# An LSTM step on one core: the new cell in PSUM for ScalarE's tanh, and a second copy of it in SBUF at the end of the step

## What is computed

```python
xW = jnp.einsum('ntd,dg->ntg', x, Wx) + b
def step(carry, xw_t):
    prev_h, prev_c = carry
    a = xw_t + prev_h @ Wh
    i = jax.nn.sigmoid(a[:, :Hdim])
    f = jax.nn.sigmoid(a[:, Hdim:2 * Hdim])
    o = jax.nn.sigmoid(a[:, 2 * Hdim:3 * Hdim])
    g = jnp.tanh(a[:, 3 * Hdim:])
    next_c = f * prev_c + i * g
    next_h = o * jnp.tanh(next_c)
    return ((next_h, next_c), next_h)
_, hs = jax.lax.scan(step, (h0, c0), jnp.swapaxes(xW, 0, 1))   # h0 is cond_1024, c0 is zero
x = x + jnp.swapaxes(hs, 0, 1)
```

## Time and profile before

| | before |
|---|---|
| median of 3 executions | 1871.62 us (1871.56 to 1872.72) |
| the profiled execution's own time | 1872.67 us |
| its span, from the first to the last instruction | 1870.8 us |
| VectorE busy | 1766.2 us, 94% |
| TensorE busy | 1691.8 us, 90% |
| ScalarE busy | 1084.4 us, 58% |
| mean granted TensorE clock | 0.999 |

### The profile page before, as it was taken

How to read it: one execution, slowest core, us unless ns; L and a number is a source line. 1 busy time by engine, 2 the same in 40 slices (tenths; PEclk the granted TensorE clock), 3 DMA queues, 4 the chain that set the end, 5 groups by cost and what they waited for, 6 DMA issues and landing times.

```text
span 1870.8 us, 104928 instructions
## 1 busy us (share of the span) xinstructions
PE 1691.8 (90%) x45116; PEld 1064.5 (57%) x45116; DVE 1766.2 (94%) x9739; ACT 1084.4 (58%) x3985; POOL 168.8 (9%) x536
## 2 busy tenths in 40 slices
PE   1899999999999999999999999999999999999997
PEld 0555555555555555555555555555555555555554
DVE  8999999999999999999999999999999999999998
ACT  4555555555555555555655555555655555556554
POOL 0000000000000000000000000000000000000000
PEclk9999999999999999999999999999999999999999
DMA  5000000000000000000000000000000000000000
GB/s 208 15 26 21 21 25 21 21 21 26 21 21 26 21 21 23 24 21 21 26 20 20 26 21 21 21 26 21 21 26 21 21 23 23 21 21 26 18 12 14
DMA packets 39058, 48.96 MB, mean 26 GB/s; under 512 B 4416, under 2 KB 36160, under 8 KB 38592
## 3 DMA queue, kind: packets, MB, share of 16 engines
q1 hardware_dynamic: 37152, 37.77, 6.4%
q10 hardware_dynamic: 1440, 4.49, 0.6%
HBM read 25.46 MB, written 16.78 MB: 23 GB/s over the span
## 4 chain that ended last, share of the span: by engine, by line
DVE 76%; PE 21%; issue 2%; DMA 1%; ACTq 0%; DVEq 0%
DVE turned L500 21%; PE acc L301 12%; DVE mailbox L504 12%; DVE products L513 10%; PE acc L307 8%; DVE o_gate L518 6%; DVE h_halves L529 4%; DVE gates L523 4%; DVE h_halves L538 4%; DVE h_feat L533 3%; DVE x_halves L483 3%; DVE out_ring L565 3%; DVE o_preact L508 3%; DVE x_tops L576 2%; DMA wh<-in_wh 1%
## 5 line engine op out<-in xcount | busy, mean ns | idle before, releaser
L301 PE MATMUL acc<-wh_low,h_halves 128*32 128x256 f16 x16384 | 719.6, 274 | 134.4 <-DVE h_halves L529 132.1
L307 PE MATMUL acc<-wh_high,h_halves 128*32 128x256 f16 x16384 | 724.9, 275 | 0.2
L250 ACT ACTIVATE gates<-mailbox 128x96 f32<-128x96 f32 x1024 | 256.3, 250 | 639.6 <-DVE mailbox L504 639.6
L293 PE MATMUL x_acc<-wx_high,x_halves 128*32 128x512 f16 x8192 | 621.0, 380 | 1.1 <-ACT x_acc L224 1.1
L301 PEld LDWEIGHTS acc<-wh_low,h_halves 128*32 128x32 f16 x16384 | 389.7, 96 | 395.0 <-DVE h_halves L529 381.8
L500 DVE STREAM_TRANSPOSE turned<-acc 128x256 f32<-128x256 f32 x1024 | 458.1, 447 | 58.0 <-PE acc L307 52.1
L307 PEld LDWEIGHTS acc<-wh_high,h_halves 128*32 128x32 f16 x16384 | 343.5, 96 | 132.4 <-DVE h_halves L538 6.8
L293 PE MATMUL x_acc<-wx_low,x_halves 128*32 128x512 f16 x4096 | 399.1, 379 | 0.0
L227 ACT ACTIVATE acc<-x_acc,step_mask 128x512 f32<-128x512 f32 x512 | 328.4, 642 | 3.9 <-PE x_acc L293 3.9
L184 POOL TENSOR_TENSOR o_preact<-turned 128x32 f32<-128x32 f32 x512 | 165.6, 323 | 1696.8 <-DVE turned L500 1696.8
L504 DVE TENSOR_TENSOR mailbox<-turned 128x96 f32<-128x96 f32 x1024 | 269.9, 264 | 17.6
(11 more groups left out here) (66 smaller groups left out, 534.8 us busy)
## 6 DMA issues: line engine op xcount, KB each, us to landing
out<-out_ring SPq DMA_DIRECT2D x128, 128.0 KB, 2.1
x_ring<-in_x SPq DMA_DIRECT2D x120, 128.0 KB, 2.9
wx<-in_wx ACTq DMA_DIRECT2D x4, 512.0 KB, 8.1
wx<-in_wx SPq DMA_DIRECT2D x4, 512.0 KB, 8.1
wh<-in_wh SPq DMA_DIRECT2D x4, 512.0 KB, 16.7
wh<-in_wh ACTq DMA_DIRECT2D x4, 512.0 KB, 17.0
x_ring<-in_x SPq DMA_DIRECT2D x2, 512.0 KB, 16.5
b_rows<-in_b ACTq DMA_DIRECT2D x1, 256.0 KB, 21.2
```

The lines of the kernel that those rows point to most:

```text
L250: act.activation(gates[par][n][:, 1:4, :], preact[n].rearrange("p (g c) b -> p g (c b)", c=2), ACT.Tanh, scale=rescale[chunk % 2]).then_in ...
L293: last = pe.matmul(x_acc[pair % 2][32 * j:32 * j + 32], x_halves[:, pair % (CHUNK // 2), c, half], w[:, c].rearrange("p (n q) g -> p q n g ...
L301: pe.matmul(acc[par][32 * j:32 * j + 32, n, 0:GL], h_halves[1 - par][:, c, 0:2], w_low["wh"][:, c, n * Q + j], start=False, stop=False, sk ...
L307: last = pe.matmul(acc[par][32 * j:32 * j + 32, n, 0:GL], h_halves[1 - par][:, c, 1:3], w_high["wh"][:, c, n * Q + j], start=False, stop=c ...
```

## The change

VectorE's new_cell now writes the cell to PSUM, into the tile `cell[n]` in `mailbox[n]`, and ScalarE's tanh reads it there. Two more VectorE instructions, `keep_cell(0)` and `keep_cell(1)`, compute the cell again from the same products and write it to SBUF, where the next step's gate_products reads it. They stand behind low_of_h(1) and ahead of the output row. They signal a new semaphore, `cell_kept`, for which gate_products(0) of the next step waits beside its wait for ScalarE. Group 1's `preact` moves to `mailbox[1]`, and the wait for `x_sum_ready` in step 6 moves up, ahead of add_three(1).

```diff
-        preact = [mailbox[0][:, 96 * n:96 * (n + 1)].rearrange("p (k b) -> p k b", b=B) for n in range(NG)]
+        preact = [mailbox[n][:, 0:96].rearrange("p (k b) -> p k b", b=B) for n in range(NG)]
+        cell = [mailbox[n][:, 128:128 + 2 * B] for n in range(NG)]
...
+        cell_kept = sem("cell_kept")
...
-                    act.activation(cell_tanh[n], gates[1 - par][n][:, 0, :], ACT.Tanh, scale=0.5)\
+                    act.activation(cell_tanh[n], cell[n], ACT.Tanh, scale=0.5)\
                         .then_inc(h_parts_ready[n], 1)
...
                 def gate_products(n):
+                    if t > 0 and n == 0:
+                        dve.wait_ge(cell_kept, NG * t)
                     dve.wait_ge(gates_ready, nth[n])
...
                 def new_cell(n):
                     dve.wait_ge(products_ready, nth[n])
+                    dve.scalar_tensor_tensor(cell[n], products[n][:, 0, :], 0.5, products[n][:, 1, :],
+                                             ALU.mult, ALU.add).then_inc(cell_ready, 1)
+
+                def keep_cell(n):
                     dve.scalar_tensor_tensor(gates[1 - par][n][:, 0, :], products[n][:, 0, :], 0.5, products[n][:, 1, :],
-                                             ALU.mult, ALU.add).then_inc(cell_ready, 1)
+                                             ALU.mult, ALU.add).then_inc(cell_kept, 1)
...
                 gate_products(0)
+                if at == 6 and chunk + 1 < CHUNKS:
+                    dve.wait_ge(x_sum_ready, chunk + 2)
                 add_three(1)
...
                 high_of_h(0)
-                if at == 6 and chunk + 1 < CHUNKS:
-                    dve.wait_ge(x_sum_ready, chunk + 2)
                 new_cell(1)
...
                 low_of_h(1)
+                keep_cell(0)
+                keep_cell(1)
```

## The result

The changed kernel takes 1949.25 us (median; 1949.13 to 1949.47), against 1871.59 for the kernel before on the same chip. The ratio is 1.0415, with a 95% interval of 1.0399 to 1.0430: 77.7 us slower, where 80.4 was forecast. The profiled execution spans 1947.7 us.

What follows compares the result with a forecast made beforehand. Each step was taken as one chain through VectorE, with ScalarE and TensorE at fixed places. The terms 35.8 - 2.2 + 46.8 + 0 = 80.4 us on 1872.67 gave 1953.1, or 1952.0 at the median; range 1930 to 1970.

Steps and rivals of the forecast that it cites:

- The chain through a step: A delay between turn(0) and low_of_h(1) lengthens the step equally; later work is free if it fits into 0.70 us.
- Four links: Late starts released by something ending just before: gate_products(0), new_cell(1), high_of_h(1) and the next step's turn(0).
- The second wait, 35.8 us: At gate_products(0), the late gates_ready becomes a separate instruction and costs 0.07 us, 511 times.
- The rival that it is free: The second wait on gate_products(0) costs nothing because VectorE's sequencer may run ahead: 1916 us, chance 0.08.
- The wait moved in step 6, -2.2 us: New_cell(1) loses its double wait, saving 0.07 us 31 times; the wait at add_three(1) costs nothing.
- The tail, 46.8 us: Two instructions behind low_of_h(1): hidden in ordinary steps; 0.21 us in steps 12-15, 0.15 in 1-4, 0.07 in 7.
- The rival that the tail fits: The 256-column operations may leave room for the two instructions behind low_of_h(1): 1905 us, chance 0.06.
- The cell in PSUM, nothing: New_cell's write of 32 columns to PSUM instead of SBUF carries no surcharge: 0 us.
- the 264 ns of the rival: New_cell's write to PSUM takes 264 ns, 76 more, adding 36 us: 1988 us, chance 0.07.
- The shorter tanh: ScalarE's tanh of the cell gets shorter reading PSUM, without gain because high_of_h(1) waits for the output gate.
- The rival that it is on the chain: High_of_h(1) waits for ScalarE's tanh, so shortening it gains 11 us: 1860 us if other costs are nothing, chance 0.02.
- The sum: 35.8 - 2.2 + 46.8 + 0 = 80.4 us added to the whole kernel, 1952.0 us predicted.

Runs made afterwards that it cites:

- the other order: The changed kernel with gate_products(0)'s two waits swapped, so that the early cell_kept is split off: 1913.31 us, ratio 1.0216.
- on top of in_gaps: in_gaps with gate_products(0)'s two waits back in the changed kernel's order, late gates_ready split off: 1908.06 us, ratio 1.0187.
- in_gaps: The changed kernel with waits swapped and both cell copies moved to where VectorE waits for its own results, cell still in PSUM: 1870.75 us, ratio 0.9988.
- alone, without the stalls: wait_only with nine tiny memsets at the head of VectorE's list: 1909.90 us, ratio 1.0197.
- sum_wait_early: The kernel before with only step 6's wait for x_sum_ready moved ahead of add_three(1): 1870.64 us, ratio 0.9987.
- wait_only: The kernel before with only a second, long since met wait added on gate_products(0), late gates_ready split off: 1912.97 us, ratio 1.0214.

## Why the prediction was right, point by point

- **The chain through a step.** Right. Four links carry it, and the experiments on two of them, the wait of gate_products(0) and the work between low_of_h(1) and turn(0), moved the time accordingly. The 0.70 from low_of_h(1) to turn(0) held in the ordinary step of the changed kernel.
- **The second wait, 35.8 us.** Right in kind, and 1 us small. Three comparisons give 37.2 (the other order), 37.1 (on top of in_gaps) and 36.9 (alone, without the stalls). Over 511 steps that is 0.072 to 0.073 each, from a term that was read as 0.07. Of the 37.2 and the 37.1, 0.4 each are eight short stalls (last section). The rival that it is free is out: 37 us hang on the order of two lines.
- **The wait moved in step 6, -2.2 us.** Right: -2.4 on its own, of which 0.4 is the stalls that went with it, and -2.1 in the kernel in_gaps.
- **The tail, 46.8 us.** The mechanism was right, and the term was 4.7 us too large: 42.1 measured. By the rows the distance from low_of_h(1) to turn(0) grows as forecast, 0.91 - 0.70 = 0.21 in the steps with L485, and not at all in steps 5, 6 and 8 to 10. What was left out is that a late turn(0) is also a little quicker: its record is 0.44 instead of 0.45, and add_three(0) starts 1007.36 - 1006.88 = 0.48 behind it, where it started 0.49 behind. A hundredth in each of 279 steps is 2.8 us. The steps with the maximum show it: from the turn at 1006.88 to the next one at 1010.62 they take 3.74, of which 3.54 is the step of before and 0.07 the wait, which leaves 0.13 where 0.15 was forecast. The trace of the kernel with the two instructions alone splits the 4.7, by the starts in nanoseconds and over all steps. From turn(0) to low_of_h(1) it is 2.5 us shorter in all than before; 0.4 of this are the four stalls in step 6 that it lacks, so about 2 remain for the quicker turn, and why it is quicker isn't shown. From low_of_h(1) to turn(0) it is 44.2 us longer in all, 2.6 less than forecast, since the sizes were each a little large: 0.203 us in steps 12 to 15 where the prediction took 0.21 (two distances of 0.10 and "their rounding"), 0.138 in steps 1 to 4 where it took 0.15, and 0.059 in step 7 where it took 0.07. The rival that the tail fits is out.
- **The cell in PSUM, nothing.** Right. The groups of the changed kernel by form, VectorE and ScalarE:

```profile
L527 DVE SCALAR_TENSOR_TENSOR mailbox<-products 128x32 f32<-128x32 f32 x1024 | 201.4, 197 | 0.2
...
L531 DVE SCALAR_TENSOR_TENSOR gates<-products 128x32 f32<-128x32 f32 x1024 | 146.4, 184 | 0.0
```

```profile
L262 ACT ACTIVATE mailbox<-mailbox 128x32 f32<-128x32 f32 x1024 | 191.8, 187 | 104.3 <-DVE mailbox L527 103.2
```

  The write to PSUM takes 197 ns where the write to SBUF took 188, 9 ns more in the record. That is far from the 264 ns of the rival. None of it reaches the time: in_gaps and sum_wait_early gain 2.1 and 2.4 us, 0.3 us apart. The Trainium skill, "Perfetto Trace Analysis", section on optimizing Scalar and DVE operations, gives VectorE's data-access overhead as about 60 ns on SBUF and 125 on PSUM, 65 apart; for this write the trace doesn't agree, by the 9 ns.
- **The shorter tanh.** It is shorter, 187 ns on average where the page of before has 199, and it changes nothing: high_of_h(1) waits for output_gate(1), which ends last, before and after. The rival that it is on the chain is out by the same pair of kernels.
- **The sum.** The parts as measured alone are 37.2 + 42.1 - 2.4 = 76.9, and the whole is 77.7. They add within 1 us. That the forecast of 80.4 came within 2.7 us of the whole is in part luck: the tail was put 4.7 us too high and the wait 1.4 too low.

## What to carry to other kernels

When an instruction waits for two semaphores, one of the waits becomes an instruction of its own; arrange that it is the one which is met early, since in this kernel the late one there cost 0.07 us each time and the early one nothing that shows. In all the places here where an instruction has two, it was the wait written last that was split off. A copy or any small piece of work is priced by where it stands: look for the places where the busiest engine waits for its own last result, and not only at its share of busy time. Before shortening an input of a join, see which of its inputs ends last.

## What the runs showed beyond that

**An early release of ScalarE.** With the tanh reading PSUM, the next instruction starts 1001.96 - 1001.87 = 0.09 after it, where it started 0.13 after the tanh at 905.84 of the earlier trace rows, by the next row of the same timeline of the kernel before:

```profile
905.97 0.58 ACT L224 ACTIVATE x_acc<-b_rows 128x512 f32<-128x512 f32 x1
```

The tanh's own record shortened by 0.02 or less. The Trainium skill, "Perfetto Trace Analysis", section on optimizing Scalar and DVE operations, gives the data-access overhead of one ScalarE instruction as about 93 ns on SBUF and 51 on PSUM, 42 ns apart, in time that the engine is busy, and says that the latency in a profile is about twice this. The distance of starts, 0.04 shorter, agrees with its 42 ns; the record, 0.02 shorter at most, doesn't agree with twice that. ScalarE had idle time in plenty here, so it is worth nothing in this kernel.

**Stalls by place in the list.** In wait_only VectorE stood still for 0.16 us ahead of an instruction with nothing to wait for, in 15 steps. They vanished when nine instructions were put at the head of the list. In all 15 the stalled instruction came directly behind the product whose late semaphore was split off, at a place 64 more than a multiple of 128 in VectorE's list. Shorter stalls stand in other kernels of this document. In the changed kernel new_cell(0) starts 0.28 behind add_three(1), where it is 0.17 elsewhere, in step 7 of 8 chunks:

```profile
138.50 0.26 DVE L506 TENSOR_TENSOR mailbox<-turned 128x96 f32<-128x96 f32 x1
138.78 0.20 DVE L527 SCALAR_TENSOR_TENSOR mailbox<-products 128x32 f32<-128x32 f32 x1
```

Such a step is 0.055 longer, 0.4 us in all, and the kernel with the late wait on top of in_gaps has the same eight. In the kernel before it is low_of_h(0) in step 6 of 4 chunks. All of these too are at a place 64 more than a multiple of 128, a few instructions behind a late wait that was split off; where no late wait is split off (in_gaps and the kernel with the moved wait of step 6) the steps of the later chunks show none. A difference of 3 us between two kernels of this length can thus come from nothing but the count of instructions ahead.
